# A decoder layer with routed experts on one core: all softmax exponentials on ScalarE, and the attention step in another order

## The chip, the cores and the metric

The kernel runs on one core of one Trainium2 chip. The metric is the device time of one execution in microseconds (us). The kernel before took 750.74 us, the median of three runs (748.93 to 753.12).

## What is computed

One decoder layer over 32 batches of 128 tokens with 128 features, all in fp32: self-attention with 16 heads of width 8 and a distance decay on the scores, a second attention against a context (features against features), a top-2 router over 8 experts with a gated hidden layer of 512, and a layer norm behind each of the three. The change touches the first softmax only:

```
scores = einsum('bhqd,bhkd->bhqk', qh, k_rec) / sqrt(d) * decay      # 16 heads, 128 x 128 each
attn   = softmax(scores, axis=-1)
out    = einsum('bhqk,bhkd->bhqd', attn, v_rec).reshape(b, s, d) @ W_o
x = layernorm(x + out)
x = layernorm(x + second_attention(x, ctx))
x = layernorm(x + experts(layernorm(x)))                             # top 2 of 8, weighted
```

## The kernel before

The program has four parts, one after the other: a block that holds both attentions, the router and the scatter of the normed rows to the experts' input (the first 395 us or so); a short block of tables; a block that runs 39 tiles of 256 rows through the experts; and a block that gathers the experts' rows and norms them. The change is in the first block.

There the 32 batches go through a pipeline that is written out by hand. Each engine has its own loop over steps `s` (lines 364, 557, 695, 870), and the rows of the loop are its work in one step, each for another batch: in TensorE's step `s`, the transposes of the probabilities are for batch `s - 1`, the second attention is for batch `s - 3`, the router for batch `s - 6`. The order of the rows is the order on the engine. Engines meet through semaphores only. A step on every engine deals with one batch's worth of work, so the time of a step counts about 32 times.

The pieces that matter, with their lines. **TensorE**: `score` (L522) makes a pair of score tiles; each of its matmuls uses 32 rows of the array and all of its columns (the trace writes 32\*128). `trans_p` (L533) transposes four heads of the exponentials. `mix` (L544) multiplies them with the values and `mix_sums` (L553) sums them, both in pieces of 128 rows by 32 columns (128\*32). All other matmuls use the whole array (128\*128): `trans_f`, `trans_x`, `trans_c` (L409, L421, L415), `keys`, `queries`, `values` (L455, L448, L460), `vp` (L429), `gram_of` (L478), `project` (L439, L440), `second_out` (L468), `second_sum` (L504 to L508), `logits` (L486) and `ranks` (L496, L497). An fp32 matmul shows as two records, a transpose as one.

**ScalarE** takes the exponentials and copies PSUM to SBUF (L586). The sixteen heads are two halves of eight. `exp_heads` (L659) takes the first half, head by head, with the negated row maximum as bias:

```
for h in range(HALF):
    done = act.activation(sc[:, slot, h, :], sc[:, slot, h, :], ACT.Exp, bias=rowmax[:, slot, h:h + 1])
```

`exp_half` (L665) takes the second half in one instruction of 128x1024, after `shift` on **GpSimd** (L320) has added the negated maximum to it:

```
pool.tensor_tensor(sc[:, slot], sc[:, slot], rowmax[:, slot, :].unsqueeze(2).to_broadcast([P, HALF, S]), ALU.add)
```

GpSimd also takes the inverse roots (L300, L308, L315), norms for the router (`router_rows`, L330, L333), adds the two one-hot rows (`choices`, L339), counts (`count`, L348), and issues the scatter of rows to the experts (`scatter`, L361, two indirect DMAs).

**VectorE** multiplies the scores with the decay (L737), takes the row maxima (L748), the statistics of the norms, the reciprocal of the sums (L754), and the router's best two. **SyncE** stores each batch's keys to DRAM (L225) and loads them back spread over four row groups (L229); `score` of the batch waits for that.

Of the kernel before, what the change touches and what calls it, by code (L numbers as in the profile page):

```python
# [26 lines left out]
ALU = mybir.AluOpType  # L27
# [9 lines left out]
def decoder_layer(nc, x, ctx_in, W_q, W_k, W_v, W_o, W_down, W_upk, W_upv, xWv, xbv, xWo, xbo,  # L37
# [30 lines left out]
    with ExitStack() as es:  # L68
# [95 lines left out]
        shifted = sem("shifted"); exped0 = sem("exped0"); exped1 = sem("exped1")  # L164
# [29 lines left out]
        first_step, last_step = -2, B + 6  # L194

        with nc.Block() as block:
# [45 lines left out]
            def _(pool):  # L242
# [121 lines left out]
                for s in range(first_step, last_step + 1):  # L364
                    if ever(s - 7): place(s - 7)
                    if ever(s - 6): tag(s - 6)
                    if ever(s): shift(s)
                    if ever(s - 3): rstd2_of(s - 3)
                    if ever(s - 7): scatter(s - 7)
                    if ever(s - 6): count(s - 6)  # L370
                    if ever(s - 3): router_rows(s - 3)
                    if ever(s - 5): choices(s - 5)
                    if ever(s - 4): rstd4_of(s - 4)
                    if ever(s - 1): rstd1_of(s - 1)
# [15 lines left out]
            def _(pe):  # L390
# [166 lines left out]
                for s in range(first_step, last_step + 1):  # L557
                    if ever(s - 6): trans_f(s)
                    if ever(s + 2): trans_x(s)
                    if ever(s - 3): trans_c(s)  # L560
                    if ever(s): score(s, 1)
                    if ever(s - 1): trans_p(s - 1, 1)
                    if ever(s + 2): keys(s)
                    if ever(s - 3): gram_of(s)
                    if ever(s - 6): logits(s)
                    if ever(s - 3): vp(s)
                    if ever(s + 2): queries(s)
                    if ever(s - 1): trans_p(s - 1, 2)
                    if ever(s - 1): trans_p(s - 1, 3)
                    if ever(s - 2): project(s)  # L570
                    if ever(s - 1): mix(s - 1, 0)
                    if ever(s - 1): mix(s - 1, 1)
                    if ever(s): values(s)
                    if ever(s - 3): second_out(s)
                    if ever(s + 1): score(s + 1, 0)
                    if ever(s - 1): mix(s - 1, 2)
                    if ever(s - 6): ranks(s)
                    if ever(s - 3): second_sum(s)
                    if ever(s - 1): mix(s - 1, 3)
# [669 lines left out]
```

## Time and profile before

| | |
|---|---|
| median of three runs | 750.74 us |
| profiled execution: its time, its span | 747.79 us, 746.1 us |
| TensorE busy (weight loads) | 573.0 us, 77% (453.1 us, 61%) |
| VectorE, ScalarE, GpSimd busy | 523.6 us, 395.0 us, 393.3 us |
| mean granted TensorE clock | 0.913 of full speed |
| attention block / experts / last norm | about 0 to 395 us / 410 to 700 us / 700 to 746 us |

The busy shares of a page are means over stages with different limits, so each stage has to be read apart. In the timeline view a row can hold several instructions (xN); its first number is where the first one starts, and a bracket at its end tells how long the engine had been idle before it and what ended that. "PE" are the matmuls, "PEld" the weight loads.

### The profile page before, as it was taken

Reading aid. Unit: us, or ns where it says so; the run is one execution under the profiler, and the core shown is the slowest. Engines: PE = TensorE matmul, PEld = TensorE weight load, DVE = VectorE, ACT = ScalarE, POOL = GpSimd, SP = SyncE. Lnnn points to the kernel's source line nnn. Section 1 sums busy time; section 2 is a strip of 40 time slices with the busy share of each in tenths; the row PEclk is TensorE's granted clock in tenths of the full one; section 3 lists DMA queues with packets and bytes.
Section 4 is the critical chain, followed back from the end, with each engine's and each line's share of the span. In section 5 each row is a group of like instructions: output and inputs, shape, how many; then the busy total and the mean of one; then the engine's idle time right before and its main releaser. Section 6 shows DMA issues by size and latency. Waiting matters only on the chain. (4 is left out here: it accounts for less than half of the span.)

```text
span 746.1 us, 18061 instructions
## 1 busy us (share of the span) xinstructions
PE 573.0 (77%) x5145; PEld 453.1 (61%) x5145; DVE 523.6 (70%) x1567; ACT 395.0 (53%) x1076; POOL 393.3 (53%) x751
## 2 busy tenths in 40 slices
PE   1599999999999999999630698888888888880000
PEld 1256777777777777777520587777777787770000
DVE  1268888888888888888323377677777677760877
ACT  1177888888888888888310344444444444440000
POOL 4073568777777777778670034334344444342444
PEclk9999999999999999999755799999999999995555
DMA  4252121212121211110000555555555555531442
GB/s 149 67 67 66 37 69 48 77 44 73 53 76 48 68 55 45 51 48 17 16 29 7 145 161 170 156 162 163 156 166 165 169 168 160 162 98 34 118 117 84
DMA packets 75650, 70.20 MB, mean 94 GB/s; under 512 B 7809, under 2 KB 58561, under 8 KB 75553
## 3 DMA queue, kind: packets, MB, share of 16 engines
q1 hardware_dynamic: 65264, 55.40, 25.4%
q0 software_dynamic: 5392, 11.01, 5.0%
q10 hardware_dynamic: 4896, 2.64, 1.2%
q8 instruction: 44, 0.72, 0.4%
q14 instruction: 54, 0.43, 0.2%
HBM read 53.85 MB, written 15.17 MB: 93 GB/s over the span
## 5 line engine op out<-in xcount | busy, mean ns | idle before, releaser
L1092 ACT ACTIVATE x2c<-ps_m,prt 128x256 f32<-128x256 f32 x117 | 55.5, 475 | 139.8 <-PE ps_m L1057 139.8
L737 DVE TENSOR_TENSOR sc<-ps_s,decay 128x512 f32<-128x512 f32 x128 | 84.7, 685 | 28.7 <-PE ps_s L522 28.4
L1068 PEld LDWEIGHTS ps_t<-wot,hid 128*128 128x128 f32 x624 | 93.3, 192 | 12.7 <-DVE hid L1128 4.0
L1043 POOL DMA_INDIRECT expert_out<-yt,dest x78 | 82.5, 1057 | 34.0 <-issue 27.8
L1055 PE MATMUL ps_m<-xg,w2t 128*128 128x256 f32 x234 | 73.9, 398 | 32.2 <-DVE hid L1124 29.3
L1068 PE MATMUL ps_t<-wot,hid 128*128 128x128 f32 x624 | 95.8, 277 | 2.7 <-DVE hid L1128 1.9
L522 PE MATMUL ps_s<-kbd,qT 32*128 32x512 f32 x256 | 75.9, 670 | 9.3 <-DMA kbd<-key_image 6.7
L586 ACT ACTIVATE pT<-ps_t 128x512 f32<-128x512 f32 x128 | 72.7, 593 | 16.7 <-PE ps_t L533 16.7
L748 DVE TENSOR_REDUCE rowmax<-sc 128x8 f32<-128x1024 f32 x64 | 78.1, 1220 | 0.4
L659 ACT ACTIVATE sc<-sc,rowmax 128x128 f32<-128x128 f32 x256 | 77.9, 390 | 0.0
L533 PE MATMUL ps_t<-ident,sc 128*128 128x128 f32 x512 | 77.1, 284 | 0.0
L533 PEld LDWEIGHTS ps_t<-ident,sc 128*128 128x128 f32 x512 | 57.2, 143 | 32.2 <-issue 30.2
L320 POOL TENSOR_TENSOR sc<-sc,rowmax 128x1024 f32<-128x1024 f32 x32 | 60.8, 1901 | 27.3 <-DVE rowmax L748 27.3
L361 POOL DMA_INDIRECT expert_in<-xhat,pos x64 | 65.2, 1019 | 15.8 <-issue 15.5
L1035 POOL COPY bot<-bo_rows 128x128 f32 x39 | 12.1, 310 | 116.0 <-DVE yt L1134 116.0
L1057 PE MATMUL ps_m<-xg,w1t 128*128 128x256 f32 x234 | 70.1, 382 | 0.0
L1124 DVE SCALAR_TENSOR_TENSOR hid<-ps_m,prt,sil 128x256 f32<-128x256 f32 x117 | 53.0, 480 | 22.9 <-ACT sil L1098 22.8
L1055 PEld LDWEIGHTS ps_m<-xg,w2t 128*128 128x128 f32 x234 | 35.8, 192 | 39.2 <-issue 32.5
L1151 DVE TENSOR_SCALAR xg<-ps_a,prt 128x256 f32<-128x256 f32 x39 | 21.2, 543 | 45.1 <-issue 40.7
L1098 ACT ACTIVATE sil<-x2c 128x512 f32<-128x512 f32 x78 | 48.3, 620 | 1.0 <-DVE x2c L1117 0.9
L1057 PEld LDWEIGHTS ps_m<-xg,w1t 128*128 128x128 f32 x234 | 45.0, 192 | 6.3
L544 PE MATMUL ps_a<-pT,vpad 128*32 128x128 f32 x1024 | 47.5, 282 | 0.0
(202 smaller groups left out, 1307.2 us busy)
## 6 DMA issues: line engine op xcount, KB each, us to landing
w2t<-in_L_ffn_W_dram SPq DMA_DIRECT2D x39, 256.0 KB, 2.7
w1t<-in_L_ffn_W_dram SPq DMA_DIRECT2D x39, 256.0 KB, 2.9
wot<-in_L_ffn_Wo_dram SPq DMA_DIRECT2D x39, 256.0 KB, 3.6
kbd<-key_image SPq DMA_DIRECT2D x32, 256.0 KB
xst<-expert_in SPq DMA_DIRECT2D x39, 130.0 KB, 2.1
g<-expert_out SPq DMA_DIRECT2D x32, 128.0 KB, 2.2
call<-in_ctx_dram SPq DMA_DIRECT2D x8, 256.0 KB, 6.5
key_image<-kT SPq DMA_DIRECT2D x32, 64.0 KB, 2.0
```

The lines of the kernel that those rows point to most:

```text
L320: pool.tensor_tensor(sc[:, slot], sc[:, slot], rowmax[:, slot, :].unsqueeze(2).to_broadcast([P, HALF, S]), ALU.add).then_inc(shifted, 1)
L361: pool.indirect_dma_start(xs_dram[:, :], bass.IndirectOffsetOnAxis(ap=pos[:, b, k:k + 1], axis=0), xhat[:, b, :], None).then_inc(scattered ...
L522: mm = pe.matmul(ps_s[:, i, :, :], qT[rows, b % 3, :], kbd[rows, b % 3, :, :], start=True, stop=True)
L533: mm = pe.transpose(ps_t[:, i % 2, j * S:(j + 1) * S], sc[:, 2 * (b % 2) + i // 2, 4 * (i % 2) + j, :], ident[:, :])
L586: return act.activation(out, in_, ACT.Copy)
L659: done = act.activation(sc[:, slot, h, :], sc[:, slot, h, :], ACT.Exp, bias=rowmax[:, slot, h:h + 1])
L737: dve.tensor_tensor(sc[:, 2 * (b % 2) + i // 2, j:j + 4, :], ps_s[:, i % 2, :, :], decay[:, :].unsqueeze(1).to_broadcast([P, 4, S]), ALU.m ...
L748: dve.tensor_reduce(rowmax[:, slot, :], sc[:, slot], AX.X, ALU.max, negate=True).then_inc((maxed0, maxed1)[half], 1)
L1043: pool.indirect_dma_start(ys_dram[:, :], bass.IndirectOffsetOnAxis(ap=dest[:, n, a:a + 1], axis=0), yt[:, par, a, :], None).then_inc(y_out ...
L1055: pe.matmul(ps_x2[c], w2t[:, par, P * c:P * c + P], xg[:, par, :], start=True, stop=True)
L1057: pe.matmul(ps_x1[c], w1t[:, par, P * c:P * c + P], xg[:, par, :], start=True, stop=True).then_inc(up, 1)
L1068: mm = pe.matmul(ps_y[par][:, a * P:(a + 1) * P], hid[:, par, c, a * P:(a + 1) * P], wot[:, par, c, :], start=(c == 0 and a == 0), stop=(c ...
```

## The change

Three edits, all in the first block.

1. `shift` on GpSimd and its semaphore go. `exp_heads` gets a second argument and takes either half, head by head, with the maximum as bias; `exp_half` goes. The row maximum of the second half now waits for the exponentials of the batch before last instead of for `shift`.
2. The rows of all four loops stand in another order, ScalarE's shifted by one step against the others (its loop has one step more: `last_step` is `B + 7`).
3. On TensorE, `mix(s - 1, 0)` and `mix(s - 1, 1)` have `queries` between them, `score(s + 1, 0)` follows `mix(s - 1, 1)`, and `mix(s - 1, 2)` and `mix(s - 1, 3)` stand together, apart from `mix_sums`.

```
-        first_step, last_step = -2, B + 6
+        first_step, last_step = -2, B + 7
...
-                def shift(b):
-                    slot = 2 * (b % 2) + 1
-                    pool.wait_ge(maxed1, b + 1)
-                    pool.tensor_tensor(sc[:, slot], sc[:, slot], rowmax[:, slot, :].unsqueeze(2).to_broadcast([P, HALF, S]),
-                                       ALU.add).then_inc(shifted, 1)
...
-                def exp_heads(b):
-                    slot = 2 * (b % 2)
-                    act.wait_ge(maxed0, b + 1)
+                def exp_heads(b, half):
+                    slot = 2 * (b % 2) + half
+                    act.wait_ge((maxed0, maxed1)[half], b + 1)
                     for h in range(HALF):
                         done = act.activation(sc[:, slot, h, :], sc[:, slot, h, :], ACT.Exp, bias=rowmax[:, slot, h:h + 1])
-                    done.then_inc(exped0, 1)
-
-                def exp_half(b):
-                    slot = 2 * (b % 2) + 1
-                    act.wait_ge(shifted, b + 1)
-                    act.activation(sc[:, slot], sc[:, slot], ACT.Exp).then_inc(exped1, 1)
+                    done.then_inc((exped0, exped1)[half], 1)
...
-                    if half == 0:
-                        before(dve, exped0, b - 1)
-                    else:
-                        before(dve, shifted, b - 1)
+                    before(dve, (exped0, exped1)[half], b - 1)
...
                     if ever(s - 3): vp(s)
+                    if ever(s - 1): mix(s - 1, 0)
                     if ever(s + 2): queries(s)
...
+                    if ever(s - 1): mix(s - 1, 1)
+                    if ever(s + 1): score(s + 1, 0)
+                    if ever(s): values(s)
```

**TensorE, a step in the middle.** Before, from `mix` 0 and 1 to the sums:

```order
L544 MATMUL ps_a<-pT,vpad 32x128 x8
L460 MATMUL ps_m<-wvf,xT 128x128
L468 MATMUL ps_m<-vpT,gA 128x128
L522 MATMUL ps_s<-kbd,qT 128x512 x2
L544 MATMUL ps_a<-pT,vpad 32x128 x4
L496 MATMUL ps_m<-both,earlier 128x8
L497 MATMUL ps_m<-cum,ones 128x8
L504 MATMUL ps_m<-xwoT,oT 128x128
L507 MATMUL ps_m<-bo_row,first 128x128
L508 MATMUL ps_m<-x,ident 128x128
L544 MATMUL ps_a<-pT,vpad 32x128 x4
L553 MATMUL ps_a<-pT,pick 32x128 x16
```

In the changed kernel the lines are some seven lower (`mix` is L537, `score` L515, `mix_sums` L546). Its first half of that stretch:

```order
L422 MATMUL ps_m<-cT,xwvT 128x128
L537 MATMUL ps_a<-pT,vpad 32x128 x4
L441 MATMUL ps_m<-xT,wq 128x128
L537 MATMUL ps_a<-pT,vpad 32x128 x4
L515 MATMUL ps_s<-kbd,qT 128x512 x2
L453 MATMUL ps_m<-wvf,xT 128x128
```

and its second half, up to the transposes of the next step:

```order
L490 MATMUL ps_m<-cum,ones 128x8
L537 MATMUL ps_a<-pT,vpad 32x128 x8
L497 MATMUL ps_m<-xwoT,oT 128x128
L500 MATMUL ps_m<-bo_row,first 128x128
L501 MATMUL ps_m<-x,ident 128x128
L546 MATMUL ps_a<-pT,pick 32x128 x16
L526 MATMUL ps_t<-ident,sc 128x128 x8
```

The same matmuls stand in another order: the 32-column work came in three groups a step (the row of 8, the row of 4, the rows of 4 and 16), and comes in four now (4, 4, 8, 16), and the group that followed the scores directly follows a whole-array matmul.

**ScalarE, a step in the middle.** Before, from the first half's exponentials on:

```order
L659 ACTIVATE sc<-sc,rowmax 128x128 x8
L677 ACTIVATE x<-ps_m,nm,rs 128x128
L586 ACTIVATE vpad<-ps_m 128x4x4x8
L665 ACTIVATE sc<-sc 128x1024
L586 ACTIVATE xfT<-ps_m 128x128
L586 ACTIVATE xT<-ps_m 128x128
L586 ACTIVATE cT<-ps_m 128x128
L586 ACTIVATE pT<-ps_t 128x512 x2
```

Now (`exp_heads` is L652, the copies L579):

```order
L652 ACTIVATE sc<-sc,rowmax 128x128 x8
L681 ACTIVATE gex,gsum<-gm,gmax 128x128
L579 ACTIVATE kT<-ps_m 128x128
L579 ACTIVATE qT<-ps_m 128x128
L620 ACTIVATE vpT<-ps_m,bv_col 128x128
L658 ACTIVATE gA<-gex,gsum 128x128
L579 ACTIVATE pT<-ps_t 128x512 x2
L579 ACTIVATE oT<-ps_m 128x128
L652 ACTIVATE sc<-sc,rowmax 128x128 x8
```

The instruction of 128x1024 became eight of 128x128, and the copy of the keys (`kT`) comes behind the first eight exponentials.

**GpSimd, a step in the middle.** Before, from `place` to `choices`:

```order
L352 CAST pos<-row_f 128x2
L343 CAST xhat<-idx 128x1
L320 TENSOR_TENSOR sc<-sc,rowmax 128x1024
L306 TENSOR_TENSOR rs<-shift,mv 128x2
L308 TENSOR_TENSOR rs<-rs,mhalf 128x2
L361 DMA expert_in<-xhat,pos 32768x130 x2
L348 TENSOR_TENSOR cum<-cum,both 128x8
L330 TENSOR_TENSOR xc<-xc,rs 128x128
L333 TENSOR_TENSOR xf<-xc,offset_row 128x128
L339 TENSOR_TENSOR both<-oh 128x8
```

Now:

```order
L337 CAST xhat<-idx 128x1
L346 CAST pos<-row_f 128x2
L333 TENSOR_TENSOR both<-oh 128x8
L355 DMA expert_in<-xhat,pos 32768x130 x2
L298 TENSOR_TENSOR rs<-mv,eps_col 128x1
L300 TENSOR_TENSOR rs<-rs,mhalf 128x1
L306 TENSOR_TENSOR rs<-shift,mv 128x2
L308 TENSOR_TENSOR rs<-rs,mhalf 128x2
L342 TENSOR_TENSOR cum<-cum,both 128x8
```

The 128x1024 row is gone, and `choices` (`both`) stands ahead of the scatter.

## Rows read from the trace of the kernel before

**Rows 1.** Windows view, three stretches of the attention block.
```profile
core 0: us, PE busy (x) PEld busy (x) DVE busy (x) ACT busy (x) POOL busy (x), PEclk, DMA share, GB/s
160.00:200.00 40.00, 40.00 (x476) 29.77 (x473) 34.78 (x106) 33.56 (x102) 30.62 (x60) 1.00 0.21 61
200.00:240.00 40.00, 40.00 (x476) 29.85 (x474) 34.81 (x108) 33.89 (x103) 30.31 (x61) 1.00 0.21 59
```
**Rows 2.** Timeline of TensorE: `score` of pair 0, at four starts.
```profile
64.27 1.13 PE L522 MATMUL ps_s<-kbd,qT 32*128 32x512 f32 x4
...
83.03 1.13 PE L522 MATMUL ps_s<-kbd,qT 32*128 32x512 f32 x4
...
204.58 0.70 PE L522 MATMUL ps_s<-kbd,qT 32*128 32x512 f32 x2
...
214.75 0.70 PE L522 MATMUL ps_s<-kbd,qT 32*128 32x512 f32 x2
```
**Rows 3.** Timeline of TensorE's weight loads, most of one step: start, length, instruction.
```profile
202.94 0.30 PEld L440 LDWEIGHTS ps_m<-xall,ident 128*128 128x128 f32 x2
203.37 0.38 PEld L544 LDWEIGHTS ps_a<-pT,vpad 128*32 128x32 f32 x16
203.94 0.30 PEld L460 LDWEIGHTS ps_m<-wvf,xT 128*128 128x128 f32 x2 [0.20 <-issue]
204.16 0.30 PEld L468 LDWEIGHTS ps_m<-vpT,gA 128*128 128x128 f32 x2
204.58 0.30 PEld L522 LDWEIGHTS ps_s<-kbd,qT 32*128 32x128 f32 x4
205.64 0.16 PEld L544 LDWEIGHTS ps_a<-pT,vpad 128*32 128x32 f32 x8 [0.76 <-issue]
206.00 0.30 PEld L496 LDWEIGHTS ps_m<-both,earlier 128*128 128x128 f32 x2 [0.20 <-issue]
...
206.88 0.30 PEld L508 LDWEIGHTS ps_m<-x,ident 128*128 128x128 f32 x2
207.31 0.16 PEld L544 LDWEIGHTS ps_a<-pT,vpad 128*32 128x32 f32 x8
207.44 0.90 PEld L553 LDWEIGHTS ps_a<-pT,pick 128*32 128x32 f32 x32
208.54 0.42 PEld L533 LDWEIGHTS ps_t<-ident,sc 128*128 128x128 f32 x4 [0.20 <-issue]
```
**Rows 4.** Timeline of ScalarE, part of one step.
```profile
204.87 2.43 ACT L659 ACTIVATE sc<-sc,rowmax 128x128 f32<-128x128 f32 x8
208.08 0.46 ACT L677 ACTIVATE x<-ps_m,nm,rs 128x128 f32<-128x128 f32 x1 [0.78 <-issue]
...
208.59 1.05 ACT L665 ACTIVATE sc<-sc 128x1024 f32<-128x1024 f32 x1
209.61 0.28 ACT L586 ACTIVATE xfT<-ps_m 128x128 f32<-128x128 f32 x1
```
**Rows 5.** Timeline of SyncE, keys of one early and one later batch.
```profile
44.38 0.56 SPq L225 DMA_DIRECT2D key_image<-kT  x1
47.49 0.52 SPq L229 DMA_DIRECT2D kbd<-key_image  x1
...
203.25 0.56 SPq L225 DMA_DIRECT2D key_image<-kT  x1
206.71 0.53 SPq L229 DMA_DIRECT2D kbd<-key_image  x1
```
**Rows 6.** Timeline of TensorE: the scores that wait for the early keys.
```profile
55.70 0.70 PE L522 MATMUL ps_s<-kbd,qT 32*128 32x512 f32 x2 [1.20 <-issue]
```
**Rows 7.** Timeline of TensorE: the last three `ranks` of the block.
```profile
378.84 0.57 PE L496 MATMUL ps_m<-both,earlier 128*128 128x8 f32 x2 [2.97 <-POOL both L339]
...
382.99 0.57 PE L496 MATMUL ps_m<-both,earlier 128*128 128x8 f32 x2 [1.82 <-POOL both L339]
...
387.19 0.57 PE L496 MATMUL ps_m<-both,earlier 128*128 128x8 f32 x2 [1.87 <-POOL both L339]
```

More of the change, by code:

```diff
@@ L163, in decoder_layer @@
         scored = sem("scored"); decayed = sem("decayed"); maxed0 = sem("maxed0"); maxed1 = sem("maxed1")
-        shifted = sem("shifted"); exped0 = sem("exped0"); exped1 = sem("exped1")
+        exped0 = sem("exped0"); exped1 = sem("exped1")
         p_trans = [sem(f"p_trans{i}") for i in range(4)]; pT_ready = [sem(f"pT_ready{i}") for i in range(4)]
@@ L364, in _ @@
                 for s in range(first_step, last_step + 1):
[L365 to L374, printed above, removed]
+                    if ever(s - 4): tag(s - 4)
+                    if ever(s - 4): place(s - 4)
+                    if ever(s - 3): choices(s - 3)
+                    if ever(s - 4): scatter(s - 4)
+                    if ever(s + 1): rstd1_of(s + 1)
+                    if ever(s): rstd2_of(s)
+                    if ever(s - 3): count(s - 3)
+                    if ever(s - 1): rstd4_of(s - 1)
+                    if ever(s): router_rows(s)
                     if s == 0:
@@ L695, in _ @@
                 for s in range(first_step, last_step + 1):
-                    if ever(s - 4): copy_vp(s - 4)
-                    if ever(s - 7): norm4(s - 7)
-                    if ever(s - 4): gram_exp(s - 4)
-                    if ever(s + 1): copy_k(s + 1)
-                    if ever(s + 1): copy_q(s + 1)
-                    if ever(s - 4): second_weights(s - 4)
-                    if ever(s - 2): copy_p(s - 2, 2)
-                    if ever(s - 2): copy_p(s - 2, 3)
-                    if ever(s - 4): copy_o(s - 4)
-                    if ever(s - 1): exp_heads(s - 1)
-                    if ever(s - 3): norm1(s - 3)
-                    if ever(s - 1): copy_v(s - 1)
-                    if ever(s - 1): exp_half(s - 1)
-                    if ever(s - 6): copy_f(s - 6)
-                    if ever(s + 2): copy_x(s + 2)
-                    if ever(s - 3): copy_c(s - 3)
-                    if ever(s - 1): copy_p(s - 1, 0)
-                    if ever(s - 1): copy_p(s - 1, 1)
+                    if ever(s - 3): copy_v(s - 3)
+                    if ever(s - 5): norm1(s - 5)
+                    if ever(s - 3): copy_p(s - 3, 0)
+                    if ever(s - 8): norm4(s - 8)
+                    if ever(s - 8): copy_f(s - 8)
+                    if ever(s - 3): copy_p(s - 3, 1)
+                    if ever(s): copy_x(s)
+                    if ever(s - 5): copy_c(s - 5)
+                    if ever(s - 2): exp_heads(s - 2, 0)
+                    if ever(s - 5): gram_exp(s - 5)
+                    if ever(s): copy_k(s)
+                    if ever(s): copy_q(s)
+                    if ever(s - 5): copy_vp(s - 5)
+                    if ever(s - 5): second_weights(s - 5)
+                    if ever(s - 3): copy_p(s - 3, 2)
+                    if ever(s - 3): copy_p(s - 3, 3)
+                    if ever(s - 5): copy_o(s - 5)
+                    if ever(s - 2): exp_heads(s - 2, 1)
             @block.vector
@@ L896, in _ @@
                     if ever(s - 4): best(s - 4)
+                    if ever(s + 2): decayed_scores(s + 2, 2)
+                    if ever(s - 1): gram_max(s - 1)
         gate1 = sb("gate1", [P, B]); gate2 = sb("gate2", [P, B])
```

36 lines of the change are left out of this document (15 added, 21 removed).

## The prediction

> **What bounds the kernel now.** I read the page's slices first, to see that the attention block, where all of the change lies, runs at full clock. Then I read the windows view of its middle: TensorE's matmuls are busy for all of 40 us in each stretch, VectorE for 34.8, ScalarE for 33.6 to 33.9, GpSimd for 30.3 to 30.6, and the granted clock is 1.00 [rows 1]. One step lasts 214.75 - 204.58 = 10.17 us [rows 2], so in a step VectorE works 8.85 us, ScalarE about 8.6 and GpSimd about 7.7. A busy TensorE alone proves little, so I looked for a test: the steps before the router's part begins (`trans_f`, `logits`, `ranks`) last (83.03 - 64.27) / 2 = 9.38 us [rows 2], 0.79 less. In the weight loads, which are the tighter row here, a whole-array matmul takes 0.22 us (from 203.94 to 204.16 [rows 3]) and a transpose half of that: one transpose and three matmuls of the router make 0.11 + 3 x 0.22 = 0.77 us. The step shrinks by just what TensorE has less to do. So its in-order queue is the bound, the other engines wait for it, and nothing that ScalarE or GpSimd saves can show in the middle of the block.
>
> Then I asked what a step of TensorE is made of, in starts of weight loads [rows 3]. Three things are to be seen. (1) A whole-array matmul to the next: 0.22. (2) A whole-array matmul to a 32-column group: 202.94 to 203.37 and 206.88 to 207.31, 0.43 each, so **entering costs 0.21**. A group of 16 loads then lasts 0.57 until the next whole-array load, and a group of 8 lasts 0.36: 8 loads are 0.21, and **leaving costs 0.15**. (3) A whole-array matmul to the scores, which use 32 rows: 204.16 to 204.58, 0.42, so entering costs 0.20; the scores take 1.06, whatever follows, and the group of 8 behind them shows no entrance of its own. The shape of the array changes nine times in a step of before.
>
> **The change part by part.**
>
> *GpSimd.* It loses 1.90 us per step and comes to 5.8 of 10.17. It was no bound: 0 us in the middle of the block.
>
> *ScalarE's exponentials.* Eight instructions take 2.43 us, of which about 0.10 overlaps the next [rows 4], so 2.33. The one that goes took 209.61 - 208.59 = 1.02. A step gains 1.31 us of ScalarE work, 8.6 + 1.31 = 9.9. What hides it is ScalarE's idle time of about 1.5 us per step, such as the 0.78 us ahead of `norm1` [rows 4]. That leaves 0.3 us of cover at the old step length and 0.6 at the new one. I cost it at 0; without its cover it is a rival below. I followed the new order by hand: when the copy of `pT` 0 may start is set by TensorE, then come the copies, the first exponentials, keys and queries, `pT` 2 and 3, then `oT`, which waits for `second_out`, then the second exponentials. Each product is ready 0.4 us or more before TensorE's queue comes to it.
>
> *VectorE.* Same instructions, 8.85 us of a step. In the new order its only long stay is the row maximum behind `gram_inv`, which waits for `gram_exp`, now behind eight exponentials. Behind it are queued the row maximum of half 1 and the decay of the next batch's scores; both have over a microsecond until they are asked for. 0 us.
>
> *TensorE's order.* The same matmuls, but the changes of shape per step go from nine to eleven. (a) `mix` 0 and 1 are split by `queries`: one more way out (0.15) and one more way in (0.21). In exchange the scores of pair 0 are now entered from a 32-column group and not from a whole-array matmul, where the 0.20 goes: +0.16. (b) `mix` 2 no longer follows the scores directly but `ranks`: one more way in, +0.21. Together **+0.37 us per step**, 10.54. The one price that no row shows is the step from a 32-column group straight to the scores. If it costs the usual 0.20 on top, the sum is +0.57; if even leaving is free there, +0.22. I take 0.37, since scores followed by a 32-column group, the nearest case, show one price and not two. Steps of this kind run from the fourth (scores at 55.70) to the last batch's, 29 of them: 29 x 0.37 = **+10.7 us** (6.4 to 16.5). The Trainium skill (TensorEngine Tiling (Array Packing), Key Properties) says that changing the tiling mode drains TensorE. By that rule each of the two added changes costs a full drain of some 0.17 us (an estimate from the warm constant in TensorE: Matmul & The Clock Gate, Single matmul latency), 0.35 per step, and the sum would be +10 in place of +10.7; the rows give unequal prices by direction, and those are what I use.
>
> *Start.* The keys' copy of a batch now comes behind eight exponentials and behind queries that TensorE does later. In the first steps the way of the keys through DRAM counts: stored at 44.38, loaded from 47.49, and the scores at 55.70 had waited 1.20 us [rows 5, 6], 11.3 us from store to use. The copy for that batch comes about 1.2 us later by the new order: **+1.2 us** (0 to 3).
>
> *Keys in the middle.* Before, 214.75 - 203.25 = 11.5 us lay between the store and the scores [rows 2, 5]. Now the copy follows `queries`, which stands less than a microsecond ahead of `score`, so the way has one step, 10.5 us. The load was issued 2 to 3.5 us after the store [rows 5] and its landing isn't shown: at most 8.0 us after issue (206.71 to 214.75). Cost 0 taken, because the DMA share is only 0.21 there [rows 1]; a rival below if it is late.
>
> *End.* Once the last batch's scores are done, `ranks` waits for GpSimd's `choices`, 2.97 + 1.82 + 1.87 us [rows 7], because `choices` stood behind the scatter and the norms. It now stands ahead of the scatter, but the next step's still waits for this step's scatter. I take **-2.5 us** (-5 to 0). ScalarE's loop has one step more, but it does the same work for each batch; 0.
>
> **Sum.** 10.7 + 1.2 - 2.5 = +9.4 us. The profiled execution took 747.79 us, so it would be 757.2; the median of the runs is 2.95 us above that execution, and I forecast the median, 750.74 + 9.4 = **760 us**. The experts' block and the last norm are not touched.
>
> **The rivals.**
>
> *Changes of shape are free where weights can be loaded early* (faster). If what looks like the price of a change is slack that the scheduler of loads takes back in another order, the two added ones cost nothing and the 0.20 ahead of the scores is saved: 29 x -0.20 = -5.8, with start and end -7.1, 743.6 us. Against it: the same 0.15, 0.20 and 0.21 come back in each step and the matmuls show no idle time. For it: the gaps of the weight loads leave 10 of 40 us [rows 1]. It decides if `queries` between `mix` 0 and 1 costs no more than its 0.22. 12%. The Trainium skill (Perfetto Trace Analysis, Identifying the Most-Contended Engine) says that matmul busy time is a poor measure of TensorE's headroom and the share of weight loads a good one. By that rule the row's 29.8 of 40 us is a TensorE with a quarter of its time to spare, and an order that fills it better would be faster; the 0.79 us of rows 2 speaks against it.
>
> *ScalarE becomes the bound* (slower). It would work 9.9 us, and its waits add up to 10.17 - 8.6, some 1.5 us a step. If they all stay, a step takes 11.4 us: 29 x 1.25 = +36, 787 us; if half stays, 10.65 us: 29 x 0.48 = +14, 765 us. It decides when ScalarE waits for more than 0.6 us per step. For it: it waits for TensorE in three places of the new order too. Against it: a wait shrinks when the engine comes later. 11%.
>
> *Keys arrive late* (slower). If store to landing takes the 11.3 us of the start in the middle too, a step takes 11.4 us, +36, 787 us. For it: the scatter now starts just as the keys are stored. Against it: the start's way is shared with the load of the parameters. 5%.
>
> *Within the noise.* The price per step is at its lower bound (+6.4), the start is free and the end gives its full 5 us: about +1.4. A measurement of this kernel can tell about 0.5% from no change, 3.75 us, and would show none here. 6%.
>
> **How the numbers follow.** My forecast has 66% (its own range, from its bounds, is 752 to 770), free changes of shape 12%, a time within the noise 6%, ScalarE 11%, the keys 5%. Below 750 lies nearly all of the first rival, above 772 the keys and about half of ScalarE's case: together some 2 in 10, so the range is 750 to 772. Faster by over 0.5%: 0.10, the first rival at its full gain. Within 0.5%: 0.12, from its lesser gains (0.02), the noise case and the low end of my own range (0.04). Slower: the rest, 0.78.
>
> **What would show it.** In the new profile TensorE's matmuls are still busy for all of the middle; the distance between the scores of pair 0 is 10.5 us (9.75 before the router's part begins); a group of 8 stands on each side of `queries`, with 0.43 us ahead of it and 0.36 us to the next; ScalarE is busy for about 9.9 us of a step; the last `ranks` wait less for GpSimd. I am wrong if the distance is 10.2 or less (changes of shape free), or if TensorE's row shows idle time ahead of an instruction that waits for ScalarE or for the load of the keys, with a step over 10.8 us.

## The result and the profile after

The changed kernel takes **756.6 us** (median of 11 runs, 753.7 to 759.4), the kernel before 749.6 (11 runs, 748.5 to 753.1): ratio 1.0087, 95% interval 1.0069 to 1.0104. That is slower by more than the 0.5% that the forecast calls measurable, and inside its range. The profiled execution took 757.16 us, its span 755.4, against 747.79 and 746.1: +9.4 us where +9.4 had been forecast; between the medians lie 7.0 us. The agreement is better than the working deserved: below, two errors of over five microseconds cancel.

The windows view of the same middle, to be held against [rows 1]:

```profile
core 0: us, PE busy (x) PEld busy (x) DVE busy (x) ACT busy (x) POOL busy (x), PEclk, DMA share, GB/s
160.00:200.00 40.00, 40.00 (x466) 28.73 (x459) 34.82 (x106) 37.44 (x128) 22.84 (x53) 1.00 0.22 61
200.00:240.00 40.00, 40.00 (x470) 29.32 (x471) 34.40 (x106) 37.41 (x128) 22.45 (x53) 1.00 0.23 61
```

TensorE's matmuls are still busy for all of the time. ScalarE rose from 33.6 to 37.4 of 40 us, GpSimd fell from 30.6 to 22.8, and VectorE stayed. The timeline of TensorE, `score` of pair 0, to be held against [rows 2]:

```profile
202.34 1.13 PE L515 MATMUL ps_s<-kbd,qT 32*128 32x512 f32 x4
...
212.69 1.13 PE L515 MATMUL ps_s<-kbd,qT 32*128 32x512 f32 x4
```

A step is 10.35 us, 0.19 longer than before (23 steps from batch 7 to 30 have a mean of 10.355 us, and of 10.167 before). The starts of `score` of pair 0 in both traces, batch by batch, and then the first matmul after the block (`count` of the experts) show where the whole difference came from:

| stretch | before | after | difference |
|---|---|---|---|
| start to the first scores (batch 0) | 28.37 | 29.56 | +1.2 |
| batch 0 to 5 | 45.28 | 44.13 | -1.15 |
| batch 5 to 7 | 19.10 | 25.11 | **+6.0** |
| batch 7 to 31, 24 steps | 243.45 | 247.72 | **+4.3** |
| batch 31 to the end of the block | 63.74 | 64.11 | +0.4 |
| all behind it (code untouched) | | | -1.4 |

(The last row cannot be read as an effect of the change: over the thirteen profiled executions of this document the time behind the block lies between 343.6 and 348.4 us, with the code there untouched.)

Most of the largest entry was in no part of the forecast. It is one step, from 73.69 to 88.80: 15.11 us, where the step ahead of it took 9.71 (63.98 to 73.69). That is 5.4 us; the other 0.6 of the 6.0 are the new order of TensorE, whose steps ahead of the long one and behind it are 9.71 and 10.00 us, where they were 9.38 and 9.72. GpSimd's timeline there:

```profile
70.32 0.99 POOL L370 DMA_DIRECT2D params<-in_L_ffn_eg_dram  x1
...
79.19 0.60 POOL L377 DMA_DIRECT2D bo_rows<-in_L_ffn_bo_dram  x1
79.77 0.25 POOL L298 TENSOR_TENSOR rs<-mv,eps_col 128x1 f32<-128x1 f32 x1
80.09 0.56 POOL L300 TENSOR_TENSOR rs<-rs,mhalf 128x1 f32<-128x1 f32 x1
```

Between the first two rows lie nine more issues of parameters, about 0.9 us each: 9.5 us in which GpSimd's in-order queue does nothing else. Behind them stands the root of the first norm (`rstd1`). ScalarE's `norm1` waits for it, and TensorE waits for `norm1`:

```profile
80.93 0.46 ACT L665 ACTIVATE x<-ps_m,nm,rs 128x128 f32<-128x128 f32 x1 [2.22 <-issue]
```
```profile
73.69 1.13 PE L515 MATMUL ps_s<-kbd,qT 32*128 32x512 f32 x4
...
81.44 0.33 PE L408 MATMUL ps_m<-ident,call 128*128 128x128 f32 x1 [2.06 <-ACT x L665]
...
81.81 1.98 PE L515 MATMUL ps_s<-kbd,qT 32*128 32x512 f32 x4
83.72 1.11 PE L526 MATMUL ps_t<-ident,sc 128*128 128x128 f32 x4
...
88.80 1.13 PE L515 MATMUL ps_s<-kbd,qT 32*128 32x512 f32 x4
```

Behind that wait the scores of pair 1 take 1.98 us and not 1.13. The windows view says why: the granted clock was 0.69 and 0.62 of full speed in two stretches of 5 us; in stretches of 1 us it reads 0.50 from 82 to 88 us, the lower of its two levels (1.2 GHz). Over the whole step TensorE idles for 2.06 us (15.11 - 13.05) and is busy for 3.34 us longer than in the step ahead (13.05 - 9.71), with about the same matmuls at a mean clock of 0.77. The low clock cost more than the wait behind which it came.

```profile
80.00:85.00 5.00, 3.56 (x12) 1.90 (x13) 3.53 (x7) 4.07 (x13) 2.96 (x8) 0.69 0.72 140
85.00:90.00 5.00, 5.00 (x33) 3.02 (x32) 2.47 (x6) 2.19 (x9) 0.00 (x0) 0.62 0.07 24
...
73.69:88.80 15.11, 13.05 (x117) 8.54 (x113) 9.50 (x22) 9.54 (x34) 9.27 (x16) 0.77 0.51 61
63.98:73.69 9.71, 9.71 (x116) 6.75 (x112) 8.08 (x20) 9.13 (x33) 5.85 (x10) 1.00 0.20 38
```

Why did the issues move? They stand in GpSimd's loop under `if s == 0`, and that line was not edited. But the change renumbered the loop: `rstd1_of(s - 1)` became `rstd1_of(s + 1)` and `router_rows(s - 3)` became `router_rows(s)`, so the step `s == 0` of GpSimd now lies two to three batches later in this work, where a norm waits behind it. Before, the issues ran from 38.6 to 48.0 us.

The timeline of weight loads, to be held against [rows 3], answers the other large entry:

```profile
200.17 0.30 PEld L479 LDWEIGHTS ps_m<-router_w,xfT 128*128 128x128 f32 x2
200.31 0.51 PEld L526 LDWEIGHTS ps_t<-ident,sc 128*128 128x128 f32 x4
200.78 0.30 PEld L422 LDWEIGHTS ps_m<-cT,xwvT 128*128 128x128 f32 x2
201.21 0.16 PEld L537 LDWEIGHTS ps_a<-pT,vpad 128*32 128x32 f32 x8
201.56 0.30 PEld L441 LDWEIGHTS ps_m<-xT,wq 128*128 128x128 f32 x2 [0.20 <-issue]
201.98 0.16 PEld L537 LDWEIGHTS ps_a<-pT,vpad 128*32 128x32 f32 x8
202.34 0.30 PEld L515 LDWEIGHTS ps_s<-kbd,qT 32*128 32x128 f32 x4 [0.20 <-issue]
203.39 0.30 PEld L453 LDWEIGHTS ps_m<-wvf,xT 128*128 128x128 f32 x2 [0.76 <-ACT qT L579]
...
204.50 0.30 PEld L490 LDWEIGHTS ps_m<-cum,ones 128*128 128x128 f32 x2
204.83 0.38 PEld L537 LDWEIGHTS ps_a<-pT,vpad 128*32 128x32 f32 x16
205.40 0.30 PEld L497 LDWEIGHTS ps_m<-xwoT,oT 128*128 128x128 f32 x2 [0.20 <-issue]
```

The forecast prices are all there around `queries`: 0.43 into the group of 8 (200.78 to 201.21), 0.35 for it and the way out, 0.42 in again, and 0.36 from the second group to the scores. So the step from a 32-column group straight to the scores, which no row of before showed, costs only the leaving. What differs is `ranks`, whose matmuls move 8 columns and not 128: from `L490` to `mix` 2 lie 0.33 us, 0.10 less than behind a matmul of 128 columns. And `logits`, also of 8 columns and now followed by transposes, takes 0.14 (200.17 to 200.31) where it took 0.22. So 0.37 - 0.10 - 0.08 = 0.19 us per step. The steps before the router's part begins bear this out: they have no `ranks` and no `logits`, and there the new order costs 0.33 us (9.71 against 9.38), close to the forecast 0.37.

### The profile page after: what moved, and what is told of

It is laid out like the page before. It is cut to its first block and busy times, and to the rows that moved or that the text cites. A ratio compares the mean times of both kernels' runs of the same rounds, so it can differ in the third digit from the quotient of the medians.

```text
span 755.4 us, 18253 instructions
## 1 busy us (share of the span) xinstructions
PE 582.9 (77%) x5145; PEld 455.3 (60%) x5145; DVE 526.0 (70%) x1567; ACT 432.4 (57%) x1300; POOL 333.5 (44%) x719
## 5 line engine op out<-in xcount | busy, mean ns | idle before, releaser
L652 ACT ACTIVATE sc<-sc,rowmax 128x128 f32<-128x128 f32 x512 | 156.3, 402 | 2.7 <-DVE rowmax L733 2.7
L1077 ACT ACTIVATE x2c<-ps_m,prt 128x256 f32<-128x256 f32 x117 | 55.5, 474 | 139.3 <-PE ps_m L1042 107.7
L515 PE MATMUL ps_s<-kbd,qT 32*128 32x512 f32 x256 | 76.8, 677 | 8.5 <-DMA kbd<-key_image 7.4
L526 PE MATMUL ps_t<-ident,sc 128*128 128x128 f32 x512 | 78.8, 288 | 0.2
L526 PEld LDWEIGHTS ps_t<-ident,sc 128*128 128x128 f32 x512 | 59.0, 149 | 31.6 <-issue 31.5
L579 ACT ACTIVATE pT<-ps_t 128x512 f32<-128x512 f32 x128 | 72.4, 600 | 6.0 <-PE ps_t L526 5.5
L537 PE MATMUL ps_a<-pT,vpad 128*32 128x128 f32 x1024 | 48.2, 286 | 0.0
L1102 DVE TENSOR_SCALAR x2c<-x2c 128x512 f32<-128x512 f32 x78 | 32.8, 421 | 6.3 <-ACT x2c L1077 6.3
```

Of the source, the lines that this page charges most:

```text
L515: mm = pe.matmul(ps_s[:, i, :, :], qT[rows, b % 3, :], kbd[rows, b % 3, :, :], start=True, stop=True)
L526: mm = pe.transpose(ps_t[:, i % 2, j * S:(j + 1) * S], sc[:, 2 * (b % 2) + i // 2, 4 * (i % 2) + j, :], ident[:, :])
L579: return act.activation(out, in_, ACT.Copy)
L1077: act.activation(x2c[:, c, :], ps_x2[c], ACT.Identity, bias=prt[:, par, 2 + CH + c:3 + CH + c]).then_inc(biased, 1)
```

## The experiments

My theory: in the middle only TensorE's order counts, at these prices; the 5.4 us are the parameters' issues in the wrong place. The rivals: ScalarE, at 37.4 of 40 us, makes the step longer; the long step has another cause; the gaps of the weight loads could be filled by an order that avoids changes of shape. Where two kernels are compared by step, the step is read from starts of `score` around 200 us.

**The parameters' issues moved ahead of the loop.**

```diff
+                pool.wait_ge(scored, 1)
+                with nc.allow_non_contiguous_dma(reason="parameters of one element per partition, once"):
+                    pool.dma_start(params[:, :, 0:1], eg.rearrange("e (p a) -> p e a", a=1)).then_inc(ld_e, 16)
...
                 for s in range(first_step, last_step + 1):
...
-                    if s == 0:
-                        with nc.allow_non_contiguous_dma(reason="parameters of one element per partition, once"):
...
```

> The changed kernel, but GpSimd's eleven DMA issues for the experts' parameters stand ahead of its loop (behind the first scores) instead of in its step 0. Theory: in the changed kernel these issues (70.3 to 79.8 us) hold up the inverse root of the next batch's norm, ScalarE's norm1 waits 2.2 us for it, TensorE idles 2.1 us and then runs its next matmuls at half pace, so that one step takes 15.1 us and not 9.7. With them early, the step from 73.7 us on takes 9.7 to 10 us and the total falls by 5.4 us, less up to 1.2 us at the start, where they now share the time with the keys: 751 to 752.5 us, ratio to the kernel before 1.002 to 1.005. Rival: that step is long for another reason (a transfer, the clock by itself); then it stays, 756 to 757 us, ratio 1.009.

Measured: 755.0 us, ratio 1.0077 (1.0054 to 1.0100). The long step is gone (9.72 in place of 15.11) and the steps of the middle are the same 10.35, so that cause is shown. The total missed the expected 751 to 752.5, because the start gave most of the gain back. Its first three steps took 7.87, 11.90 and 10.64 us (7.26, 10.89 and 7.61 in the changed kernel), 4.7 us more. In the second of them `score` waits 3.58 us. The profile names no releaser; by the code its keys are what is left to wait for, and the DMA engines, which load the parameters at the same time, are busy for 0.60 of this step in place of 0.10. In the third TensorE does not idle, but the granted clock is 0.68:

```profile
48.48 2.08 PE L515 MATMUL ps_s<-kbd,qT 32*128 32x512 f32 x4 [3.58 <-issue]
```

Batch 7 came at 97.22, only 1.6 us ahead of the changed kernel's 98.80. So the block of eleven issues is not free at the start either: 4.7 us there, probably with transfers in the way of the keys, and with the clock falling behind the wait, and 5.4 us in the long step, as a hold of the queue. The -1.15 of batches 0 to 5 fits this, since the parameters of the kernel before loaded at that time, but no run separates it.

**Only the split of two `mix`, in the kernel before.**

```diff
                     if ever(s - 1): mix(s - 1, 0)
-                    if ever(s - 1): mix(s - 1, 1)
                     if ever(s): values(s)
+                    if ever(s - 1): mix(s - 1, 1)
```

> The kernel before with one row of TensorE's loop moved: values stands between mix 0 and mix 1. Nothing else changes. Theory (each change of the array's shape has a price that nothing hides): one more way out (0.15) and one more way in (0.21), 10.17 + 0.36 = 10.53 us from scores to scores, 29 x 0.36 = +10.4 us, 760 us, ratio 1.014. Rival (shapes are free where weights can be loaded early, the changed kernel's longer step has another cause): 10.17 us, 749.6 us, ratio 1.000.

Measured: 757.81 us, ratio 1.0123 (1.0097 to 1.0150), a step of 10.50. Two lines of code exchanged, no instruction added or removed, cost 0.33 us in each step. The weight loads show the price twice, 0.42 in and 0.36 or 0.35 out:

```profile
207.96 0.30 PEld L440 LDWEIGHTS ps_m<-xall,ident 128*128 128x128 f32 x2
208.38 0.16 PEld L544 LDWEIGHTS ps_a<-pT,vpad 128*32 128x32 f32 x8
208.74 0.30 PEld L460 LDWEIGHTS ps_m<-wvf,xT 128*128 128x128 f32 x2 [0.20 <-issue]
209.16 0.16 PEld L544 LDWEIGHTS ps_a<-pT,vpad 128*32 128x32 f32 x8
209.51 0.30 PEld L468 LDWEIGHTS ps_m<-vpT,gA 128*128 128x128 f32 x2 [0.20 <-issue]
```

**The opposite edit in the changed kernel: `queries` ahead of `mix` 0.**

```diff
-                    if ever(s - 1): mix(s - 1, 0)
                     if ever(s + 2): queries(s)
+                    if ever(s - 1): mix(s - 1, 0)
                     if ever(s - 1): mix(s - 1, 1)
```

> The changed kernel with queries ahead of mix 0 instead of between mix 0 and mix 1. Theory (shapes): one way out and one way in less, 10.35 - 0.36 = 9.99 us per step, which ScalarE with 9.7 us of work can just follow: 29 x 0.36 = -10.4 us, 746 us, ratio 0.996. Rival (ScalarE holds the step of the changed kernel): the step stays near 10.35 us, 756 us, ratio 1.009.

Measured: 746.61 us, ratio 0.9967 (0.9947 to 0.9987). A step is 10.02, ScalarE at 38.68 of 40 us, TensorE still at 40.00:

```profile
200.00:240.00 40.00, 40.00 (x476) 29.85 (x468) 35.64 (x108) 38.68 (x133) 23.31 (x57) 1.00 0.23 60
```

ScalarE does the same work in a step that is 0.33 us shorter, so it did not set the 10.35; 29 steps of 0.33 are 9.6 us, and the kernel is 10.0 us faster than the changed one. (By the traces 7.4 us of this are the 24 steps from batch 7 on, 0.9 the start, and 1.4 the long step, in which the clock fell less.) With its change of shape taken back, the changed kernel's steps are shorter than those of before, and the kernel is within the 0.5% of it although its long step (here 13.68 us) remains.

**Only the exponentials, in the order of before.** GpSimd's subtraction is out and all sixteen heads have their own exponential, but no loop is reordered.

```diff
-                    if ever(s): shift(s)
...
-                    if ever(s - 1): exp_heads(s - 1)
+                    if ever(s - 1): exp_heads(s - 1, 0)
                     if ever(s - 3): norm1(s - 3)
                     if ever(s - 1): copy_v(s - 1)
-                    if ever(s - 1): exp_half(s - 1)
+                    if ever(s - 1): exp_heads(s - 1, 1)
```

> The kernel before with the exponentials as in the changed kernel (shift gone, both halves head by head with the bias) in the old order of all loops. Theory (TensorE bounds the step, ScalarE has 1.5 us of idle time per step and gets 1.3 more work): ScalarE is nearly full, the distance of the scores is 10.2 to 10.5 us, total +0 to +10 us, 750 to 760 us. Rival (ScalarE's waits do not shrink in the old order and the new order was needed for them): 10.8 us or more per step, 768 us or more.

Measured: 767.19 us, ratio 1.0235 (1.0208 to 1.0263), a step of 10.66 to 10.71: between the two expectations. ScalarE is busy for only 36.29 us, and TensorE now waits for its copy `xT`, once a step:

```profile
200.00:240.00 40.00, 39.06 (x462) 28.80 (x461) 32.80 (x103) 36.29 (x123) 21.20 (x55) 1.00 0.20 55
```
```profile
200.26 0.49 PE L448 MATMUL ps_m<-xT,wkf 128*128 128x128 f32 x2 [0.23 <-ACT xT L579]
```
```profile
210.03 0.42 PEld L526 LDWEIGHTS ps_t<-ident,sc 128*128 128x128 f32 x4 [0.76 <-issue]
210.92 0.30 PEld L448 LDWEIGHTS ps_m<-xT,wkf 128*128 128x128 f32 x2 [0.47 <-ACT xT L579]
```

The weight load of `keys` starts 0.89 us behind that of the four transposes, where it was 0.39 in the kernel before: this one place holds all of the 0.5 us.

So the load that I costed at 0 is free only in the new order. The edit of the exponentials alone costs 0.5 us a step, and the reordering that came with it takes 0.3 of them back, although it has two more changes of shape.

**The reverse: the new order, with the subtraction and the single exponential of half 1 back.**

```diff
-        first_step, last_step = -2, B + 7
+        first_step, last_step = -3, B + 7
...
-                    if ever(s - 4): scatter(s - 4)
+                    if ever(s + 3): shift(s + 3)
                     if ever(s + 1): rstd1_of(s + 1)
                     if ever(s): rstd2_of(s)
+                    if ever(s - 4): scatter(s - 4)
...
-                    if ever(s - 2): exp_heads(s - 2, 1)
+                    if ever(s - 2): exp_half(s - 2)
```

> The changed kernel's order on TensorE, ScalarE and VectorE, but with GpSimd's subtraction back (ahead of the inverse roots, the scatter behind them) and the second half's exponentials in one instruction. ScalarE loses 1.3 us of work per step. Theory (TensorE's order alone makes the step of 10.35 us, the exponentials' engine costs nothing): 10.35 us from scores to scores, total 754 to 758 us, ratio 1.006 to 1.011. Rival (part of the longer step is ScalarE's extra load): 10.2 us or less, 751 us or less.

Measured: 763.51 us, ratio 1.0181 (1.0128 to 1.0233). The step is the same 10.35 with ScalarE at 32.81 us and not 37.41:

```profile
200.00:240.00 40.00, 40.00 (x467) 28.79 (x464) 35.00 (x108) 32.81 (x102) 29.58 (x60) 1.00 0.20 58
```
```profile
203.69 1.13 PE L522 MATMUL ps_s<-kbd,qT 32*128 32x512 f32 x4
...
214.04 1.13 PE L522 MATMUL ps_s<-kbd,qT 32*128 32x512 f32 x4
```

In the new order neither ScalarE's load (1.2 us a step by these rows, where the forecast had 1.31) nor the 1.90 us of GpSimd is worth anything in the middle. The total came out above what was expected: the long step is 16.47 us here (TensorE waits 3.96 us, since the subtraction, 1.95 us, stands in GpSimd's queue too), and from the last batch's scores to the end of the block it takes 70.57 us, not 64.11. The cause of the second was not isolated.

**`ranks` earlier.** If `ranks` in front of `mix` 2 makes entering cheaper, taking it away must cost 0.10.

```diff
+                    if ever(s - 6): ranks(s)
                     if ever(s - 2): project(s)
                     if ever(s - 3): second_out(s)
-                    if ever(s - 6): ranks(s)
                     if ever(s - 1): mix(s - 1, 2)
```

> The changed kernel with ranks moved ahead of project, so that mix 2 and 3 follow second_out (128 moving columns) and not ranks (8 moving columns). Theory (the way into the 32-column shape is dearer, 0.21 instead of 0.11, when the matmul ahead of it moves 128 columns): 10.45 us from scores to scores instead of 10.35, total +3 us on the changed kernel, 759 to 760 us, ratio 1.012 to 1.014. Rival (the missing 0.1 us of the changed kernel's step lies elsewhere): 10.35 us, ratio 1.009.

Measured: 762.23 us, ratio 1.0161 (1.0121 to 1.0201). The way in is 0.42 again:

```profile
204.86 0.30 PEld L461 LDWEIGHTS ps_m<-vpT,gA 128*128 128x128 f32 x2
205.28 0.38 PEld L537 LDWEIGHTS ps_a<-pT,vpad 128*32 128x32 f32 x16
```

The step is 10.51, so 0.06 more than that price explains, and the total is 2 us above the expected. The rest sits at `gram_of`, whose weight load starts 0.45 to 0.46 us behind the transposes' and not 0.39; what it waits for was not isolated. The price is shown.

**`queries` first, and the parameters' issues spread**, one per step of GpSimd.

```diff
-                    if s == 0:
...
+                    if 4 <= s < 4 + 3 + 2 * CH:
+                        k = s - 4
...
+                                pool.dma_start(params[:, :, k:k + 1], src.rearrange("e (p a) -> p e a", a=1)).then_inc(ld_e, 16)
...
+                    if ever(s + 2): queries(s)
                     if ever(s - 1): mix(s - 1, 0)
-                    if ever(s + 2): queries(s)
```

> The changed kernel with queries ahead of mix 0, and the eleven issues for the experts' parameters one in each of eleven steps of GpSimd, behind its other work, instead of all in its step 0. Theory: the step stays at 10.02 us, the one long step (13.7 us) falls to about 9.4, and the keys' loads of the start meet no crowd: 4.3 us less than with queries ahead alone, about 742.5 us, ratio 0.991. Rival (the issues cost in whatever step they stand): 746 us or more.

Measured: **738.82 us, ratio 0.9881 (0.9825 to 0.9937)**, faster than both kernels. The step from 70.57 to 79.96 that was long is 9.39, and no norm waits for its root. At the start the scores at 52.86 still wait 1.51 us. Batch 7 comes at 89.63, where it came at 98.80 in the changed kernel and at 92.75 before:

```profile
79.96 1.13 PE L513 MATMUL ps_s<-kbd,qT 32*128 32x512 f32 x4
...
89.63 1.13 PE L513 MATMUL ps_s<-kbd,qT 32*128 32x512 f32 x4
...
99.65 1.13 PE L513 MATMUL ps_s<-kbd,qT 32*128 32x512 f32 x4
```

The gain on the run with `queries` first is 7.8 us, more than the 4.3 that were expected. By the traces the stretch up to batch 7 is 5.9 us shorter. Another 1.8 lie between the last scatter's issue and the next block, 5.4 us in each of the four runs with spread issues and 7.2 in the others; why was not isolated.

**All of `mix` in one group.** The exponentials of before, but all four loops reordered so that the scores, `mix` 0 to 3 and their sums follow each other: five changes of shape per step.

```diff
+                    if ever(s + 1): score(s + 1, 0)
                     if ever(s - 1): mix(s - 1, 0)
                     if ever(s - 1): mix(s - 1, 1)
-                    if ever(s): values(s)
...
                     if ever(s - 1): mix(s - 1, 2)
                     if ever(s - 1): mix(s - 1, 3)
                     if ever(s - 1): mix_sums(s - 1)
+                    if ever(s): values(s)
```

> The kernel before with its exponentials and its subtraction on GpSimd, and all four loops in a new order: on TensorE the scores of pair 0 are followed at once by mix 0 to 3 and the sums, and all whole-array matmuls stand together, so that the shape changes five times a step instead of nine. By the measured prices (0.20 into the scores twice, 0.15 out of the one 32-column group) that is 0.55 us of changes instead of 1.27: theory 10.17 - 0.72 = 9.45 us per step, 29 x 0.72 = -21 us, 729 us, ratio 0.972. Rival (another engine or a chain of waits now bounds the step, ScalarE with 8.6 and VectorE with 8.85 us of work and their waits): 9.9 us or more per step, 741 us or more.

Measured: 774.63 us, ratio 1.0352 (1.0292 to 1.0411), the slowest but one, with steps of 10.6 to 10.9 us. TensorE is no longer busy throughout, and its waits name ScalarE:

```profile
200.00:240.00 40.00, 37.61 (x459) 28.72 (x458) 37.31 (x102) 32.10 (x100) 28.86 (x57) 1.00 0.21 60
```
```profile
207.72 0.46 PE L504 MATMUL ps_m<-xwoT,oT 128*128 128x128 f32 x2 [0.55 <-ACT oT L586]
```

The order saves four changes, but some products are now asked for before the chain through the other engines has brought them, and that costs more than the changes. The idle rows come to about 0.6 us of a step that is 1.2 us longer than expected. What the rest is was not isolated: all four loops were reordered at once, and VectorE, busy for 37.31 of 40 us here, is as near to its limit as TensorE (the last section has one reason).

**The same with the issues spread**, one per step from GpSimd's step 7 on.

```diff
-                    if s == 0:
...
+                    if 7 <= s < 7 + 3 + 2 * CH:
+                        k = s - 7
...
```

> As the run with one 32-column group, and the eleven issues for the parameters one in each of eleven steps of GpSimd from its step 7 on instead of all in step 0. In the kernel before they lay where no norm waited for them, but shared the first steps with the keys' loads. Theory: 1 to 2 us less than with one group alone. Rival (GpSimd's work with the subtraction leaves no room for 0.9 us more in a step): equal or slower by up to 5 us.

Measured: 779.92 us, ratio 1.0410 (1.0349 to 1.0470). The steps that carry an issue take 11.35 us in place of 10.6 to 10.9, one takes 14.34. So in this kernel, with the subtraction in GpSimd's queue, an issue costs about 0.7 us in the step that carries it; in the faster kernel above it costs nothing. By busy time GpSimd would have room here too (28.86 of 40 us without the issues), so it is again a matter of what waits behind the issue, and that was not isolated.

**A middle way: `mix` 2, 3 and the sums joined** in the fastest kernel, seven changes of shape.

```diff
+                    if ever(s - 3): second_out(s)
                     if ever(s - 2): project(s)
-                    if ever(s - 3): second_out(s)
                     if ever(s - 6): ranks(s)
+                    if ever(s - 3): second_sum(s)
                     if ever(s - 1): mix(s - 1, 2)
                     if ever(s - 1): mix(s - 1, 3)
-                    if ever(s - 3): second_sum(s)
```

> The kernel with queries ahead of mix 0 and spread parameters, in which second_out comes first behind values and second_sum ahead of mix 2, so that mix 2, mix 3 and the sums are one 32-column group: seven changes of shape per step. Theory (shapes): 0.15 + 0.21 less, 0.10 more for the dearer way in, 10.02 - 0.26 = 9.76 us per step if ScalarE, with 9.7 us of work, keeps up; total 29 x 0.26 = 7.5 us less, 731 us, ratio 0.978. Rival (ScalarE bounds now, or second_sum waits for the copy of oT): 10.0 us per step, 738 us or more.

Measured: 745.44 us, ratio 0.9935 (0.9911 to 0.9958). The step is 10.11, longer than the 10.02 that it started from and 0.35 above the expected 9.76. The windows view has TensorE busy for 39.78 of 40 us, but the starts of the weight loads show where it loses the 0.35: ahead of `second_out`, now directly behind `values` (0.35 us from one to the other, 0.21 between `values` and `project` before), ahead of the transposes of the norm's output (0.96 behind the eight of the exponentials, 0.83 before) and ahead of `gram_of` (0.48, 0.39 before). So the changes of shape saved what they were priced at, and waits of about 0.1 us each, which hardly show as idle time, took more than that back. The norm's output comes late:

```profile
205.33 0.46 ACT L663 ACTIVATE x<-ps_m,nm,rs 128x128 f32<-128x128 f32 x1 [0.49 <-issue]
```

**The same with the last norm's scaling on GpSimd**, to relieve ScalarE.

```diff
-                    if ever(s - 8): norm4(s - 8)
...
+                    if ever(s - 2): norm4(s - 2)
```

(The first is ScalarE's loop, the second GpSimd's.)

> As the run with the joined sums, and the last norm ahead of the router's scatter (norm4) on GpSimd instead of ScalarE, which takes 0.38 us per step off ScalarE and gives GpSimd some 0.5. Theory: where ScalarE holds the step above 9.76 us, this brings it there, 731 us or less. Rival (GpSimd's in-order queue delays the roots behind it): no gain on the joined sums or a loss of several us.

Measured: 746.13 us, ratio 0.9942 (0.9923 to 0.9960), a step of 10.1 to 10.3. ScalarE's busy time fell from 37.89 to 36.71 us of the stretch from 160 to 200 and nothing was gained. (One step, from 213.09 to 224.94, takes 11.85.) So ScalarE's busy share was not the limit; that the arrival of its inputs is fits the row above, but was not tested by itself.

## Why the prediction was right, and where it was not

- *What bounds the kernel.* Right. TensorE was and is busy throughout, and in the run with the new order and the old exponentials the step stays at 10.35 with 4.6 us of 40 less on ScalarE. That the gaps of the weight loads were no time to spare is shown by the two runs that move one row: with the same matmuls the step went up by 0.33 us and down by 0.33. (The one-group order, which tried to use those gaps, lost by waits, and proves nothing about them.) The share of weight loads, 29.85 of 40 us, is the same in the kernel of before and in the one with `queries` first, whose step is 0.15 shorter: here that share does not rank them.
- *TensorE's order, +0.37 per step, +10.7 in all.* Right in kind, but the term was mis-sized: 0.37 where 0.19 was measured. The term "one more way in, +0.21" for `mix` 2 behind `ranks` took the price from rows in which a matmul of 128 columns stood ahead. Behind 8 columns it is 0.11. That `logits` would be 0.08 cheaper ahead of transposes was not looked at. Measured: 0.19 per step, +4.3 over the 24 steps from batch 7 on, and with +0.33, +0.33 and +0.28 in the three ahead of them +5.2 in all. The part around `queries`, with a price that no row of before showed, came out as taken; the run with `queries` moved confirms it with 0.33 per step.
- *GpSimd, 0 us.* This is the step that failed. "It was no bound" looked at the busy time of a step in the middle, and the moves were counted there. The eleven issues under `s == 0` did not appear in the diff as moved, and they were moved by two to three steps all the same: +5.4 us in one step, 2.06 of waiting and 3.34 of low clock. Only the runs that moved them, ahead of the loop and spread, say that they are the cause.
- *ScalarE, 0 us.* Right, but on a condition worth more than the sentence gave it: in the old order the same edit costs 0.5 us a step, and not by ScalarE's load as a whole, for it idles there too, but by one copy that comes late. The cover was made by the reordering.
- *Start, +1.2.* The first scores are 1.2 us later, as forecast, but by batch 5 this is gone (-0.3 without the price of the changes). That the parameters no longer load beside the keys would explain it, but is not shown.
- *Keys in the middle, 0.* Right: stored at 202.53, the scores wait for nothing.
- *End, -2.5.* Measured +0.4. The waits of the last three `ranks` [rows 7] did shrink, by 1.8 us together, as the tail of TensorE's timeline shows:

```profile
389.37 0.57 PE L489 MATMUL ps_m<-both,earlier 128*128 128x8 f32 x2 [1.43 <-POOL both L333]
...
393.87 0.57 PE L489 MATMUL ps_m<-both,earlier 128*128 128x8 f32 x2 [2.17 <-POOL both L333]
...
397.43 0.56 PE L489 MATMUL ps_m<-both,earlier 128*128 128x8 f32 x2 [1.23 <-POOL both L333]
```

  But counted from the last batch's scores (336.20 before, 346.52 now), the five `ranks` ahead of these come 0.6 to 1.6 us later than before, so the last one stands at 50.9 and before at 51.0: the waits shrank and nothing was gained. The last scatter of GpSimd, which the next block waits for, is even issued 0.4 us later, 55.9 us behind those scores and before 55.5. The rows are the one of before, then the one of now:

```profile
391.74 0.97 POOL L361 DMA_INDIRECT expert_in<-xhat,pos  x1 [0.30 <-issue]
```
```profile
402.45 0.97 POOL L355 DMA_INDIRECT expert_in<-xhat,pos  x1 [0.30 <-issue]
```

  The step that failed is to count the idle time of TensorE in front of `ranks` as time that the block would lose. Which chain sets the pace of the block's end was not isolated.
- *The rivals.* Free changes of shape: refuted, also by the split alone (+1.2% for two exchanged lines). ScalarE as the bound: not in this kernel; in the old order TensorE does wait for it, though it is busy for only 36.29 of 40 us. Late keys: not in the middle; at the start they are the likely cause of a wait of 3.58 us, in the run whose parameters load early.

Put together: the steps gave 5.2 for 10.7, the start -0.3 for 1.2, the end +0.4 for -2.5, the issues 5.4 and the code behind the block -1.4 for nothing: 9.3 in place of 9.4. That the sums agree is luck.

## What to carry to other kernels

When a change renumbers the steps of a hand-written pipeline, look for everything that is tied to a step's number and is not in the diff: a block of eleven DMA issues moved in this way cost as much here as all the changes of shape. Spread such one-time issues over several steps, and look at each whether something waits behind them: this gained 7.8 us in one kernel of this document and lost 5.3 in another. And on a TensorE that is busy throughout, an order is compared by its changes of array shape, priced by what stands directly ahead of each, but only as long as every product is still there when it is asked for.

## What the runs showed of the hardware

- Changing TensorE's shape has prices by direction, and the way into a 32-column group depends on what is ahead: 0.20 to 0.21 us behind matmuls of 128 columns, 0.11 behind one of 8 columns; 0.15 out; from a 32-column group to the 32-row scores only the way out. The Trainium skill (TensorEngine Tiling (Array Packing), Key Properties) says that the array drains at a change; the rows agree that each change costs, except the one from the scores to any other shape, which shows no price of its own; a drain that is shorter behind a shorter matmul would fit, but was not shown.
- A wait of 2.06 us of TensorE cost 5.4 us, because the granted clock fell behind it to a mean of 0.77 over the step. The length of the wait alone does not give the price: in the run with `ranks` earlier a wait of 2.03 us in the same place cost 3.9 us (a step of 13.58, 9.72 ahead of it, mean clock 0.87), and with `queries` first one of 2.36 cost 4.3 (13.68, 9.39 ahead, 0.88).
- An instruction of VectorE with two inputs in SBUF was held here until one of GpSimd on SBUF had ended. In the one-group kernel a 128x16 operation took 1.30 us, beside the subtraction of 1.90 us:

```profile
203.04 1.30 DVE L853 TENSOR_TENSOR oh<-iota_e,idx 128x16 f32<-128x16 f32 x1
```
```profile
202.42 1.90 POOL L320 TENSOR_TENSOR sc<-sc,rowmax 128x1024 f32<-128x1024 f32 x1 [0.25 <-DVE rowmax L748]
```

  It ends with the subtraction, at 204.3. In the kernel before, the same operation takes 0.17 us, apart from the subtraction, and VectorE's whole time rose from 34.8 to 37.3 of 40 us in the one-group kernel, though its steps are longer; this operation alone is 1.1 us a step. The Trainium skill (SBUF — State Buffer, Who interferes with whom) says that a VectorE instruction with two SBUF inputs contends with a GpSimd instruction that reads SBUF, and calls the shared port pair an exclusive lock; these rows agree.
